# Graph attention on one core: eleven tiles a layer fetched row by row from SyncE instead of gathered by GpSimd

## The reference

```python
q = (xp @ Wq[l] + bq[l]).reshape(n, H, HD)      # H = 8 heads of HD = 16
k = (xp @ Wk[l] + bk[l]).reshape(n, H, HD)
v = (xp @ Wv[l] + bv[l]).reshape(n, H, HD)
att = jnp.einsum('ehd,ehd->eh', q[dst], k[src]) / scale
att = jnp.nan_to_num(jnp.clip(att, -50.0, 50.0), nan=0.0, posinf=50.0, neginf=-50.0)
m = jax.ops.segment_max(att, dst, num_segments=n)
ex = jnp.exp(att - m[dst])
s = jax.ops.segment_sum(ex, dst, num_segments=n)
alpha = ex / (s[dst] + 1e-16)
msg = (v[src] * alpha[:, :, None]).reshape(-1, D)
aggr = jax.ops.segment_sum(msg, dst, num_segments=n)
x = x + (aggr @ Wo[l] + bo[l])
h = jax.nn.gelu(_layernorm(x, ln2_g[l], ln2_b[l]) @ W1[l] + b1[l], approximate=False)
x = x + (h @ W2[l] + b2[l])
```

## Time and profile before

| what | value |
|---|---|
| median of three runs | 2799.0 us |
| lowest, highest run | 2790.19, 2799.18 us |
| profiled execution: span from first to last instruction | 2183.8 us |
| profiled execution: whole time | not given on its page; the span is 615.2 us short of the median of the runs |
| GpSimd busy | 1570.6 us, 72% of the span |
| VectorE busy | 1710.2 us, 78% |
| TensorE busy | 1419.8 us, 65% |
| ScalarE busy | 940.2 us, 43% |
| DMA queues, share of 16 engines | software 33.8%, hardware 10.3% |

### The profile page before, as it was taken

One profiled execution on the slowest core, in us unless ns is written; L12 is line 12 of the kernel. 1 busy time (PEld: TensorE's weight loads), 2 busy tenths in 40 slices (PEclk: granted clock), 3 DMA queues, 4 the chain that ended last, 5 costly groups with the idle time before them and its releaser, 6 DMA issues.

```text
span 2183.8 us, 32409 instructions
## 1 busy us (share of the span) xinstructions
PE 1419.8 (65%) x8227; PEld 1237.3 (57%) x8227; DVE 1710.2 (78%) x5103; ACT 940.2 (43%) x2179; POOL 1570.6 (72%) x1669
## 2 busy tenths in 40 slices
PE   4866576666667676766666657566666757666666
PEld 4555565656555565655556556556555656555555
DVE  8759888888877878787877777777777778777775
ACT  8334353534535353534454335343343435343344
POOL 6277777777777777777727777777777777777773
PEclk9979888877878788887988787787787778787787
DMA  2365445444444444444424444444444444444441
GB/s 87 119 178 182 148 133 154 147 136 134 142 134 125 142 134 142 124 142 134 132 69 143 135 125 136 137 123 139 133 139 124 139 134 129 134 134 138 125 138 56
DMA packets 123505, 289.29 MB, mean 132 GB/s; under 512 B 31525, under 2 KB 57057, under 8 KB 123329
## 3 DMA queue, kind: packets, MB, share of 16 engines
q0 software_dynamic: 77824, 212.31, 33.8%
q1 hardware_dynamic: 45504, 74.92, 10.3%
HBM read 275.44 MB, written 8.38 MB: 130 GB/s over the span
## 4 chain that ended last, share of the span: by engine, by line
POOL 47%; issue 20%; DVE 11%; PE 11%; DMA 6%; ACT 3%; DVEq 1%; SPq 0%; ACTq 0%
POOL kvr L801 47%; DMA kvr<-kv_table,srcidx 5%; PE bank L1079 4%; PE bank L1092 3%; DVE agg L1706 3%; DVE kvr L1322 2%; DVE prod L1675 1%; DVE msg L1697 1%; ACT apart L1279 1%; ACT onehotT L1283 1%; DVE onehot L1667 1%; PE bank L1036 1%; PE bank L1015 1%; PE bank L816 1%; PE bank L894 1%
## 5 line engine op out<-in xcount | busy, mean ns | idle before, releaser
L801 POOL DMA_INDIRECT kvr<-kv_table,srcidx x1612 | 1530.7, 950 | 547.4 <-issue 480.0
L1079 PE MATMUL bank<-q,onehotT 128*128 x3320 | 606.8, 340 | 712.1 <-DVE prod L1675 475.2
L1079 PEld LDWEIGHTS bank<-q,onehotT 128*128 128x128 f32 x3320 | 515.6, 237 | 825.5 <-issue 824.8
L1092 PE MATMUL bank<-msg,onehot 128*128 128x136 f32 x3320 | 612.3, 344 | 1.9 <-DVE msg L1697 1.9
L1289 ACT ACTIVATE bank<-attc 128x32 f32<-128x32 f32 x404 | 81.2, 201 | 1145.7 <-DVE attc L1691 1145.0
L1092 PEld LDWEIGHTS bank<-msg,onehot 128*128 128x128 f32 x3320 | 571.8, 252 | 3.6 <-DVE msg L1697 3.3
L1675 DVE TENSOR_TENSOR prod<-kvr,bank 128x512 f32<-128x512 f32 x404 | 276.0, 683 | 302.6 <-DMA kvr<-kv_table,srcidx 264.0
L1706 DVE TENSOR_TENSOR agg<-agg,bank 128x136 f32 x1624 | 469.1, 289 | 44.9 <-PE bank L1092 40.1
L1279 ACT ACTIVATE apart<-relT,minus_p 128x512 bf16<-128x512 bf16 x416 | 293.8, 706 | 4.4 <-DMA relT<-rel_table 4.0
L1667 DVE TENSOR_TENSOR onehot<-bank,rel 128x512 f32<-128x512 f32 x416 | 282.5, 682 | 0.2
L1697 DVE TENSOR_TENSOR msg<-kvr,bank 128x512 f32<-128x512 f32 x404 | 273.9, 678 | 5.0 <-ACT bank L1289 4.9
(11 more groups left out here) (217 smaller groups left out, 844.5 us busy)
## 6 DMA issues: line engine op xcount, KB each, us to landing
relT<-rel_table SPq DMA_DIRECT2D x104, 512.0 KB, 4.1
kvr<-kv_table,srcidx POOLq DMA_INDIRECT x1612
loop_kv<-kv_table SPq DMA_DIRECT2D x25, 128.0 KB, 3.9
kv_table<-qkv SPq DMA_DIRECT2D x25, 128.0 KB, 3.2
kv_table<-onehot SPq DMA_DIRECT2D x8, 256.0 KB, 2.2
w<-weights SPq DMA_DIRECT2D x2, 840.0 KB, 7.4
loops<-x_in SPq DMA_DIRECT2D x5, 320.0 KB, 5.6
q<-qkv SPq DMA_DIRECT2D x25, 64.0 KB
```

What stands on the lines that cost most here:

```text
L801: pool.indirect_dma_start(kvr[:, n % RING, j, :], None, kv_table[l], bass.IndirectOffsetOnAxis(ap=srcidx[:, step:step + 1], axis=0)).then_ ...
L1079: mm = pe.matmul(bank[2][:, j * D:(j + 1) * D], onehotT[:, m % OHT, j, :], q[:, bass.ds(ranks[j + h], 1), :].rearrange("p a c -> p (a c)") ...
L1092: mm = pe.matmul(sum_ps(n, k), onehot[:, m % OH, j, :], msg[:, n % 2, j, :], start=(m, j) == of[0], stop=(m, j) == of[-1])
```

## The change

SyncE now fetches the last tile of groups 31, 47, 63, ... 191 of each layer (`ROWED`, 11 groups), one row of k and v a DMA. A tile has 128 rows, fetched in 16 slots of 8 rows (`fetch_tile_rows`); tile g occupies slots g-22 to g-7, so the eleven stand end to end in slots 9 to 184. The node numbers come from a row in SBUF, `srcrow`, filled in the prelude by eleven DMAs, eight at a time into registers. A row goes to `rowkv`, which has two buffers and a gap of four numbers between k and v, so that a row is written as two pieces of 512 B. GpSimd leaves these tiles out (`pooled`). In these groups VectorE's product with k and its product with v are each split into one instruction for three tiles and one for the last, the first of which also waits for the rows.

```diff
+ROWED = tuple(range(31, 192, 16))
+ROWS_A_SLOT, ROWS_LEAD, ROW_BUFS = 8, 6, 2
+ROW_SLOTS = P // ROWS_A_SLOT
+ROW_LOAD = 8
...
+def pooled(n):
+    return gathers(n) - is_rowed(n)
...
+        rowkv = sb("rowkv", [P, ROW_BUFS, 2, D + 4])
+        srcrow = sb("srcrow", [1, len(ROWED) * P], I32)
...
+            sp.wait_ge(s_rows, 16 * 2 * SC)
+            for i, g in enumerate(ROWED):
+                chunk, step = divmod(row_of(g, at_begin=True) + G - 1, P)
+                sp.dma_start(srcrow[0:1, i * P:(i + 1) * P], step_src[step:step + 1, chunk * P:(chunk + 1) * P]).then_inc(s_srcrow, 16)
...
+            def fetch_tile_rows(l, g, part):
+                n = l * GROUPS + g
+                i = rowed_no(n)
+                if part == 0:
+                    if i >= ROW_BUFS:
+                        before = (i - ROW_BUFS) // len(ROWED) * GROUPS + ROWED[(i - ROW_BUFS) % len(ROWED)]
+                        sp.wait_ge(s_msg, before + 1)
...
+                for p0 in range(part * ROWS_A_SLOT, (part + 1) * ROWS_A_SLOT, ROW_LOAD):
+                    at = ROWED.index(g) * P + p0
+                    nodes = nc.values_load_multi_w_load_instructions(srcrow[0:1, at:at + ROW_LOAD], engines=(ENG.SP,), min_val=0, max_val=NP - 1,
+                                                                     skip_runtime_bounds_check_because="the number of a node")[1]
+                    for j, node in enumerate(nodes):
+                        sp.dma_start(rowkv[p0 + j:p0 + j + 1, i % ROW_BUFS, :, 0:D], kv_table[l][bass.ds(node, 1), :].rearrange("a (h c) -> a h c", h=2)).then_inc(s_rowkv[i % ROW_BUFS], 16)
...
+                    for g in ROWED:
+                        if 0 <= s - (g - ROWS_LEAD - ROW_SLOTS) < ROW_SLOTS:
+                            fetch_tile_rows(l, g, s - (g - ROWS_LEAD - ROW_SLOTS))
...
-                for j in range(gathers(n)):
+                for j in range(pooled(n)):
...
-                t = gathers(n)
-                dve.tensor_tensor(prod[:, 0:t, :], kvr[:, n % RING, 0:t, 0:D], ...).then_inc(s_prod, 1)
+                t = pooled(n)
+                ins = dve.tensor_tensor(prod[:, 0:t, :], kvr[:, n % RING, 0:t, 0:D], ...)
+                if is_rowed(n):
+                    i = rowed_no(n)
+                    dve.wait_ge(s_rowkv[i % ROW_BUFS], 16 * P * (i // ROW_BUFS + 1))
+                    ins = dve.tensor_tensor(prod[:, t, :], rowkv[:, i % ROW_BUFS, 0, 0:D], bank[2][:, t * D:(t + 1) * D], ALU.mult)
+                ins.then_inc(s_prod, 1)
```

## The result

The changed kernel takes 3746.0 us (median of four runs, 3740.1 to 3753.3) against 2798.1 us before (four runs beside them): a ratio of 1.340, 95% interval 1.337 to 1.343. I had forecast 2773 us, no more than 2865. The profiled execution took 3753.3 us and its span is 3751.5, so only 1.8 us lie outside the span.

The account below looks back on a forecast made before the run. GpSimd's unbroken gathers were taken as the bound: 27.6 us saved, less 2 us margin, other additions hidden, gave 2158 us of span; with 615.2 us outside it kept constant, 2799.0 - 26 = 2773 us, range 2763 to 2865.

Parts of the forecast that it names:

- What bounds the kernel: GpSimd's gathers run without a break in both layers, four making a slot of 5.01 us; VectorE and SyncE have room.
- my 4.94: GpSimd's slot after the change, 4.94 us on average, taken as the time allowed to SyncE a slot.
- My third rival: Row DMAs and added instructions lengthen the time outside the profiled span, by 20 to 170 us; chance 0.04.
- What is taken off: GpSimd drops 22 gathers at 1.254 us, all on the path: 27.6 us, 13.8 a layer.
- VectorE and the prelude: VectorE's split products add 6.6 us, hidden by waiting; eleven prelude copies on SyncE take 6 to 8 us, counted as nothing.
- The row DMA: SyncE issues one row every 0.53 us, with 0.50 as lowest and 0.90 as the far end.
- The load of eight: SyncE loads eight node numbers into registers in one access, 0.33 us with its gap.
- The rival of two: SyncE's load of eight numbers takes two accesses, 0.60 us; part of the case that the gain is eaten, chance 0.22.
- the fourth rival: SyncE's numbers cost one by one: eight take 1.66 us, the kernel about 3165 us; chance 0.06.
- The sum p: SyncE's time a slot in the first layer: 8 x 0.53 + 0.33 + 0.28 = 4.85 us, against 4.94 allowed.
- 239.4 + 175 p: Time in us of the first layer's group 201 when SyncE sets the pace; no gain lost while p < 4.93.
- Rival 2: SyncE becomes the bound, `relT` loads queue behind the rows and ScalarE's spread waits: 2878 us; chance 0.20.

Follow-up runs that it names:

- The second profile: The kernel before, unchanged, profiled again: 2799.6 us, with a span of 2797.9 us.
- the block load: The changed kernel with a tile's 128 row DMAs and their number loads replaced by one DMA of a fixed 128-row block: 2736.0 us, ratio 0.979.

## Why the prediction was wrong

**What bounds the kernel.** "GpSimd runs without a break in both layers", a slot of 5.01 us, was read correctly from the profile, and that profile is not of what is timed. "The median of the runs is 615.2 us more than the span, for which no row accounts. I keep it constant" was the first step that failed. The missing time was inside the span, as waits, so nothing let me carry it as a constant. The second profile has 6.4 us a slot, which would have left SyncE more room than my 4.94; this step alone would not have brought the loss. My third rival (0.04) put the growth outside the span, where 1.8 us lie.

**What is taken off.** 27.6 us for 22 gathers was too little: 60 us with the block load.

**VectorE and the prelude.** The extra products took 281 ns each (44 of them, estimated at 0.28 us). The block load has them and the eleven copies too and was still 60 us faster, so neither shows as a cost. These held.

**The row DMA.** "I take 0.53, the row nearest to it" was wrong: 0.75 us apart, of which the DMA is 0.562 and the registers and gaps 0.19. The nearest rows had one piece for each partition, contiguous; the one-piece row (0.228 us, 0.41 to 0.45 apart) is even cheaper than they are. My bounds were 0.50 and 0.90, and the value lies inside.

**The load of eight.** "One access, 0.33" was wrong: without gathers it took 0.525 to 1.10 us, 1.04 in the median. The rival of two, 0.60, was near what it takes behind a DMA other than a row or `relT` (0.53), and had no term for what a row DMA just ahead adds to it (0.5). Nor was it 1.66, so the fourth rival is out. The Trainium skill, "Runtime: NRT & Kernel Launch", section "Instruction fetch mechanics", has about 200 ns a register, also in bulk; an estimate by it gives 1.6 us for eight, and the trace disagrees (0.53 to 1.10 us).

**The sum p.** With the two sizes set right, p is 8 x 0.75 + 1.04 + 0.28 = 7.3 us, as measured without gathers (7.31), and my formula 239.4 + 175 p gives 1517 us for group 201 of the first layer, where that run has 1580.4. Half of these 63 us is the start, for the rows began at 218.4 us there and not at 184.7. (In the second layer 1193.8 + 7.4 + 47.3 is 1248.5, not 1246, so its limit was p < 5.23.) So the form of the sum held and its terms were too small. It fell short by what it had no term for at all: beside gathers the same slot took 9.3 us. This is the step that made the forecast wrong: p was 4.85 in it, 7.3 undisturbed and 9.3 in the changed kernel, and either measured value is above the 6.4 us of a slot of the kernel before.

**Rival 2** had the mechanism, `relT` behind the rows, and a chance of 0.20 with 0.03 more for a row of 0.90 us, "p would be 7.8 and the time some 3700 us". That the time came near this is chance: p was 9.3 and the base different. **Rival 3's** remark on the DMA engines held, though its 5632 packets were 11,616 more by the page (57,120 against 45,504): the hardware queue took 6.3% of 16 engines' span with them. With sixteen pieces a row it had 135,968 packets and the kernel was 200 us faster than with two, so packets weren't the price.

**What was missing** is a price for issuing a DMA beside gathers. SyncE's own instructions stretch there from 0.03 to as much as 1.6 us, and the signals of other engines arrive late. Of the 948 us that the change cost, going by the runs, about 220 (3048 against 2828) come from SyncE's undisturbed pace, though the run without gathers has no gather cost in it at all, and some 700 from the gathers beside it. The two aren't additive parts of one sum: with room on SyncE the rows cost 287 us, and where SyncE is the bound each stretched instruction is on the path.

**What stays open.** Why a gather's landing holds up signals and SyncE's instructions, whether the length of a burst matters, why the first profile shows almost none of it, and what a shorter lead gains. The first profile's granted clock was also higher (0.81 against 0.685), and without gathers it was 0.866. A low clock alone doesn't make `agg` wait: it waited 10.9 us at 0.667 with bursts forced to four, and 156.0 at 0.722 without gathers beside rows of two pieces. How much of the time between 2736 and 2043 us is the clock's and how much the held-up signals', no run separates.

## What to carry to other kernels

If the profiled span is far from the timed median, the profile is of another execution: take a second one before costing anything on it, and never carry the difference as a constant. Here work moved to an idle engine was paid by its instructions (25 a slot, eight of them DMAs) and by the shape of each DMA (one contiguous run 0.228 us, two pieces 0.562), not by its bytes (a block of 128 rows 0.553). Price what it does to the others too: here a tile of 128 row DMAs costs 128 x 0.022 to 0.036 = 2.8 to 4.6 us of held-up time in the cheapest form tried, and the gather that it saves is worth 2.7.

## What the runs showed of the hardware that I had not expected

- A row DMA on SyncE beside GpSimd's indirect gathers lengthens the kernel by 0.02 to 0.11 us though SyncE has room, and in its one-piece form by nothing without gathers (2041.0 against 2042.6 us).
- The time to issue a DMA depends on the shape and isn't monotonic in the pieces: 0.228 us for one run of 1024 B, 0.562 for two of 512 B, 0.506 for sixteen of 64 B, 0.666 for eight rows of two pieces, 0.553 for 128 rows of two.
- A register load of eight numbers took 1.04 us right behind a row DMA of two pieces, 0.73 behind a load of `relT` and 0.53 behind one of `loop_kv`, at the same line of one kernel.
- The same kernel gave a span of 2183.8 us in one profile and 2797.9 us in another; every timed run was near the second.
